# V of two key chunks in the two halves of one PSUM bank, with one copy, in the first cross attention of a four-layer kernel

## The reference

```
nx = layernorm(x)
q = nx @ w_q + b_q;  k = ctx @ w_k + b_k;  v = ctx @ w_v + b_v      # ctx: 375 x 192, v: 375 x 256
weights = softmax(q k^T / 4)                                        # per head
x = x + (weights v) @ w_o + b_o
```

## Time and profile before

| what | value |
|---|---|
| median of 3 runs | 2268.0 us (2265.51 to 2269.77) |
| the profiled execution's own time | 2281.14 us |
| its span, first to last instruction | 2279.3 us |
| mean granted TensorE clock | 0.972 |
| first cross attention within it | about 0 to 608 us |
| two consecutive steps of it | about 35.1 us |

### The profile page before, as it was taken

How to read it: one execution, slowest core, us unless ns; L and a number is a source line. 1 busy time by engine, 2 the same in 40 slices (tenths; PEclk the granted TensorE clock), 3 DMA queues, 4 the chain that set the end, 5 groups by cost and what they waited for, 6 DMA issues and landing times. The chain is left out here.

```text
span 2279.3 us, 60245 instructions
## 1 busy us (share of the span) xinstructions
PE 2103.6 (92%) x20227; PEld 1594.5 (70%) x20228; DVE 1407.3 (62%) x3682; ACT 1036.6 (45%) x2466; POOL 891.5 (39%) x1479
## 2 busy tenths in 40 slices
PE   5999999999599999959999999959999999999996
PEld 4777777777477777736666666646777777777774
DVE  4666666667368888752223222224877878787785
ACT  2444444444344545412222222225666666666663
POOL 3344444444146666510000000015666656656651
PEclk9999999999899999969999999977999999999998
DMA  6222322234130000021101011120111101111000
GB/s 178 78 75 76 100 76 75 75 96 177 38 128 21 24 20 21 24 73 34 34 33 32 32 32 32 35 80 24 31 34 30 37 26 38 34 30 36 28 28 9
DMA packets 98789, 118.79 MB, mean 52 GB/s; under 512 B 9778, under 2 KB 91442, under 8 KB 98610
## 3 DMA queue, kind: packets, MB, share of 16 engines
q1 hardware_dynamic: 92594, 103.43, 14.8%
q0 software_dynamic: 6144, 14.69, 2.2%
HBM read 67.36 MB, written 50.72 MB: 52 GB/s over the span
## 5 line engine op out<-in xcount | busy, mean ns | idle before, releaser
L1263 ACT ACTIVATE e_act_T<-ps_quad,fc_b 128x128 f32<-128x128 f32 x504 | 136.8, 382 | 359.2 <-PE ps_quad L1330 359.2
L479 DVE TENSOR_REDUCE a_negmax<-ps_turned 112x2 f32<-112x750 f32 x256 | 240.2, 938 | 62.7 <-PE ps_turned L569 61.0
L422 ACT ACTIVATE a_probsT<-ps_quad 125x896 f32<-125x896 f32 x192 | 176.2, 918 | 127.7 <-PE ps_quad L581 123.7
L1353 PE MATMUL ps_out<-w,e_act_T 128*128 x1008 | 229.8, 381 | 2.5 <-ACT e_act_T L1263 2.4
L1337 PE MATMUL ps_quad<-w,e_xT 128*128 x504 | 228.6, 597 | 0.9 <-DVE e_xT L1298 0.9
L1451 POOL COPY c_index<-slot 112x1 uint32 (+1 forms) x64 | 19.4, 331 | 525.8 <-POOLq L1226 525.8
L1293 DVE COPY e_pre<-ps_quad 128x1024 f32<-128x1024 f32 x63 | 77.2, 1225 | 226.4 <-PE ps_quad L1337 226.4
L1353 PEld LDWEIGHTS ps_out<-w,e_act_T 128*128 128x128 f32 x1008 | 187.9, 191 | 26.7 <-issue 3.5
L1478 POOL TENSOR_TENSOR c_kL<-c_kT,c_kH 128x376 fp32r<-128x376 f32 x128 | 126.4, 987 | 175.3 <-ACT c_kH L1530 174.6
L206 ACT ACTIVATE c_probs<-ps_quad,c_negmax 112x375 f32<-112x375 f32 x256 | 144.1, 571 | 29.2 <-DVE c_negmax L167 29.2
L1337 PEld LDWEIGHTS ps_quad<-w,e_xT 128*128 128x128 f32 x504 | 91.5, 192 | 92.8 <-issue 92.8
(11 more groups left out here) (306 smaller groups left out, 5422.8 us busy)
## 6 DMA issues: line engine op xcount, KB each, us to landing
slots<-a_zeros SPq DMA_DIRECT2D x60, 512.0 KB, 4.9
a_cT<-in_ctx_t SPq DMA_DIRECT2D x32, 375.0 KB, 3.6
c_cT<-in_ctx_t SPq DMA_DIRECT2D x32, 375.0 KB, 3.2
w<-in_fc_t SPq DMA_DIRECT2D x2, 4096.0 KB, 21.0
w<-in_fc_t SPq DMA_DIRECT2D x8, 1024.0 KB
e_xg<-slots SPq DMA_DIRECT2D x63, 128.0 KB, 2.0
slots<-e_y SPq DMA_DIRECT2D x63, 128.0 KB, 1.7
out<-c_fo SPq DMA_DIRECT2D x32, 112.0 KB, 1.9
```

The costliest lines, as they stand in the source:

```text
L422: act.activation(probsT[t][:, c, :, :], turned[0:KC, :, 0:HALF], ACT.Exp).then_inc(exp_ready, 1)
L479: dve.tensor_reduce(negmax[:, t, e, :].rearrange("p (r c) -> p r c", c=32)[:, 2 * half:2 * half + 2, 0], plain[0:T, :, 0:CTX], AX, ALU.max ...
L1263: last = act.activation(act_T[:, c * TILE:(c + 1) * TILE], hidden_T[:, c // 4, (c % 4) * TILE:(c % 4 + 1) * TILE], ACT.Gelu, bias=b1[:, ba ...
L1353: last = pe.matmul(y_ps[:, 0:D], act_T[:, c * TILE:(c + 1) * TILE], w2[:, bass.ds(e, 1), c, :].rearrange("p a d -> p (a d)"), start=(c == ...
```

## The change

The V product of chunk 1 moves on TensorE from behind plain(0, 3) to directly behind the product of chunk 0, and writes columns 256 to 511 of the same bank. Only the second of the two products increments `v_mm`, by two. On VectorE one instruction, `v_copy_two`, in the place of the copy of chunk 0, takes both halves of the bank out (125 x 512 elements) and increments `v_ready` by two. The copy of chunk 1 at the end of VectorE's step goes, and so does TensorE's wait for the first copy. Chunk 2 keeps its product and its copy.

```diff
+                def v_copy_two(b, to):
+                    dve.wait_ge(v_mm, 3 * b + 2)
+                    wait(dve, values_ready, 2 * (b - 1))
+                    dve.tensor_tensor(v[to][:, 0:2, :, 0:HD], proj[0:KC, :].rearrange("p (c h d) -> p c h d", c=2, h=H),
+                                      bv[0:KC, :].rearrange("p (h d) -> p h d", h=H).unsqueeze(1).to_broadcast([KC, 2, H, HD]), ALU.add)\
+                       .then_inc(v_ready, 2)
...
                         maximum(nxt, 0, 1)
-                        v_copy(nxt, 1 - par, 0)
+                        v_copy_two(nxt, 1 - par)
...
                         maximum(nxt, 0, 3)
-                        v_copy(nxt, 1 - par, 1)
...
                     def v_product(of, c):
                         keys = slice(c * KC, (c + 1) * KC)
-                        chain(pe, proj[0:KC, 0:D], [...]).then_inc(v_mm, 1)
+                        to = proj[0:KC, 0:D] if c != 1 else proj[0:KC, D:2 * D]
+                        return chain(pe, to, [...])
...
-                        v_product(par, 2)
+                        v_product(par, 2).then_inc(v_mm, 1)
...
                         v_product(1 - par, 0)
+                        v_product(1 - par, 1).then_inc(v_mm, 2)
...
                         plain_scores(1 - par, 0, 3)
-                        pe.wait_ge(v_ready, 3 * nxt + 1)
-                        v_product(1 - par, 1)
                         pe.wait_ge(max_ready, 8 * nxt + 4)
                         shift_turn(1 - par, 0)
```

More of the change, by code:

```diff
@@ L561, in v_product @@
                         keys = slice(c * KC, (c + 1) * KC)
-                        chain(pe, proj[0:KC, 0:D], [(cH[of][:, 0, keys], wvH[:, 0, :]), (cH[of][:, 0, keys], wvL[:, :]), (cL[of][:, 0, keys], wvH[:, 0, :]),
-                                                         (cH[of][:, 1, keys], wvH[:, 1, :]), (cL[of][:, 1, keys], wvH[:, 1, :])]).then_inc(v_mm, 1)
+                        to = proj[0:KC, 0:D] if c != 1 else proj[0:KC, D:2 * D]
+                        return chain(pe, to, [(cH[of][:, 0, keys], wvH[:, 0, :]), (cH[of][:, 0, keys], wvL[:, :]), (cL[of][:, 0, keys], wvH[:, 0, :]),
+                                              (cH[of][:, 1, keys], wvH[:, 1, :]), (cL[of][:, 1, keys], wvH[:, 1, :])])
                     def plain_scores(of, t, u):
```

## The result

The changed kernel takes 2323.07 us (median of four runs, 2317.37 to 2323.33), the kernel before 2268.89 us (2265.51 to 2272.78): a ratio of 1.0232, 95% interval 1.0209 to 1.0255. That is 54 us slower, where 21 were forecast and the range ended at 2297. The profile is of a run of 2322.87 us.

The account below looks back on a forecast made before the run. TensorE and VectorE, neither full, bound the kernel by waiting in turns. 29 steps at 0.64 us (18.6), 2.2 for b = -1 and 0, and 0.2 for b = 30 gave +21 on 2268.0: 2289 us, range 2276 to 2297.

Parts of the forecast that it names:

- relay: End of a step: TensorE and VectorE take turns, so a late copy delays max(0, 2), then plain(0, 3), by 0.64 us.
- Step 1: On VectorE, the double copy must wait for both products and starts 0.51 us later, 0.04 behind the last matmul.
- Step 2: The 512-element double copy on VectorE takes 0.69 us, 0.27 more than the single copy; bounds 0.42 and 0.84.
- Steps 3 to 5: max(0, 2) is 0.78 us late, plain(0, 3) waiting for it 0.64 late; `apply` adds no further loss.
- the sum: Whole stage: 18.6 us for steps 1 to 29, 2.2 for b = -1 and 0, about 0.2 for b = 30; +21.
- The cover over TensorE's own lateness: The 0.24 to 0.45 us that five earlier matmuls delay TensorE is hidden, since plain(0, 3) waits longer for VectorE.
- I cost their removal at nothing: End of TensorE's step: removing five matmuls worth 0.58 us gains nothing, as the shift turn waits for max(0, 3).
- a gap of about 1 us: Before the shift turn, TensorE's time without loads grows from 0.46 to about 1 us.
- the clock falls: Rival: the longer gap before the shift turn halves the granted clock, costing 43 us, 2332 us or more; chance 0.02.

Follow-up runs that it names:

- e3: Changed kernel with the layer-norm moments moved ahead of the double copy on VectorE; 2302.94 us, ratio 1.0124 to the kernel before.
- e4: Changed kernel with the double copy split into two of 256 elements, the second at the end of VectorE's step; 2302.96 us, ratio 1.0127.
- e6: Kernel before with five more, unused V matmuls ahead of the product of chunk 0; 2291.63 us, ratio 1.0079.
- e1: Changed kernel with five unused V matmuls added behind plain(0, 3), filling the gap; 2302.25 us, ratio 1.0114 to the kernel before.
- e2: Kernel before with the V product of chunk 1 left out, so its V is wrong; 2287.62 us, ratio 1.0044.
- e5: Changed kernel, unaltered, run again beside the kernel before; 2327.68 us, ratio 1.0241.
- e10: Changed kernel with two unused matmuls between `values` and plain(0, 3), the long gap left; 2316.83 us, ratio 1.0196 to the kernel before.
- e9: Changed kernel with two unused matmuls behind plain(0, 3), in the gap under max(0, 3); 2303.57 us, ratio 1.0132 to the kernel before.
- e11: Changed kernel with five filler matmuls behind plain(0, 3) and two adjacent 256-element copies replacing the double copy; 2294.87 us, ratio 1.0113 to the kernel before.
- e8: Kernel before with k product 0 moved ahead of plain(1, 3) and k product 1 ahead of the shift turn; 2269.32 us, ratio 0.9986.
- e12: Repeat of the kernel before with k product 0 ahead of plain(1, 3) and k product 1 before the shift turn; 2265.46 us, ratio 0.9981.
- e7: Changed kernel with the moments ahead of the double copy and five filler matmuls under max(0, 3); 2292.44 us, ratio 1.0078 to the kernel before.

## Why the prediction was wrong

- **The direction and one of two mechanisms** were right: slower, by the relay copy, max(0, 2), plain(0, 3). plain(0, 3) was released by the maximum and every step carried the delay on. That explains 23.5 of the 54 us.
- **Step 1, the start of the copy,** was mis-sized. I had 0.51 us later. Counted from product 0's first load it went from 0.97 to 1.54 us in one parity of the step and from 0.99 to 1.63 in the other, so 0.57 to 0.64: the wide copy follows its last matmul by 0.08 us in the step shown (224.18 + 0.28 to 224.54), and not by the 0.04 us taken from the narrow one.
- **Step 2, its duration,** was right: 0.69 us, 32 times, as interpolated.
- **Steps 3 to 5** follow: plain(0, 3) is late by 0.70 us in the step shown, and a step is 0.76 longer in the mean of two; forecast 0.64. Times 31, that is 23.5 us, where the sum had 21. The cover over TensorE's own lateness was as described, at the upper of its two bounds: 0.46 (e3, e4, e6), not 0.24.
- **"I cost their removal at nothing" is the step that failed.** The five matmuls under max(0, 3) weren't on the path, but they were TensorE's only work there. Without them it had nothing to load for 1.29 us, and the granted clock fell to half for some 7 us, six or seven times in the loop. e1, which puts five matmuls back, prices this at 22 to 30 us, about as much as the lateness. I wrote a gap of about 1 us, by adding 0.58 to 0.46; rows 4 had the right length, from the end of the loads of plain(0, 3) at 216.55 + 0.17 = 216.72 to the shift turn at 218.02, 1.30 us, since the 0.18 us ahead of product 1 becomes part of it.
- **The rival "the clock falls"** stood in the text with a chance of 0.02. I priced it only as a clock at half for the whole stage, and argued against it from waits of 0.7 us that did no harm. Those waits told nothing of one of 1.3 us. A clock that falls now and then was the case to price. Nothing on record before the result gave the number of falls; with the six or seven that came, at 3 us each, the forecast would have been about 2309.
- **The sum after the fact.** In the profiles the end of the stage moved by 48 us (608.3 to 656.4): 23.5 of lateness, 18 of six falls, and some 6 of falls at the end of the stage, which e1 and e6 have as well and whose cause no run shows. The stages behind were 6 us shorter than in the profile of before, so the spans differ by 41.7 us. The medians differ by 54; the profile of before is of a run 12 us above its median. Where the rest of the difference lies is not shown.

What stays open: what sets the number of falls. e2, e3, e4, e5 and e10 all have a gap of 1.29 us, and their profiles show 3, 2, 1, 7 and 5 falls. The changed kernel waits another 0.42 to 0.54 us before plain(0, 3), which e2, e3 and e4 don't; but e10 doesn't have all of that either and still falls five times. A single profile each is too little to say more. Nor is it separated whether the length of the gap counts or how little TensorE does around it: e9's matmuls do something to both, and e10's, which leave the gap as it is, took off some 9 us as well.

## What to carry to other kernels

Work that hides under a wait may still be what keeps TensorE's clock up: before it is moved away, look how long TensorE will then stand with nothing to load, and price a fall of the clock apart from the path. A copy merged over two products starts when the second is done, and everything queued behind it on that engine moves too; here the merged copy itself saved nothing (e1 against e11). Where a wait can't be avoided, a product may be put under it; in e8 and e12 that gave 3 to 4 us of the 9 expected.

## What the runs showed of the hardware

- One fall of the granted clock, about 7 us at 0.50 in the middle of a full-speed loop, costs 3.0 us (39.66 against 36.64 us for two steps).
- A gap of 0.46 us a step brought no fall in the loop (before, e1, e6, e7, e11), one of 0.82 a single one (e9), one of 1.29 one to seven in some 500 us. All 25 falls between 60 and 580 us began 0.8 to 2.0 us behind the load that ended this gap.
- At the start of the kernel before, the granted clock reads 1.00, but V matmuls start 0.21 us apart and last 0.41 us, as they do where it reads 0.50. That slow start lasted to between 56 and 59 us there (V matmuls from 59.26 on start 0.12 us apart). It may be what varies between executions: the first context load inside the loop is issued at 68.60 us in the kernel before and at 61.36 in e8, too much for their steps to differ by.
